# A decoder layer on one core: the folding of the cross-attention weights split between the front and the first tiles, and the order of the front rewritten

## The reference, cut to what matters

```python
x = _layernorm(x + attn(x))            # attn(x) = softmax(rope(q) rope(k)^T * s) v @ w_proj + b_proj + x
# cross attention of the tokens to the context, scale and shift by one number per batch and head
xn = layernorm(ctx, ln1_w, ln1_b); ln = layernorm(x, ln2_w, ln2_b)
q = (ln @ Wq) * (1 + side) + side; k, v = split(xn @ Wkv)
x = _layernorm(x + softmax(q k^T / 8) v @ Wout)
x = _layernorm(x + ffn(x))
```

## Time and profile before

| | us |
|---|---|
| median of 3 runs | 1294.25 |
| lowest, highest | 1291.96, 1299.49 |
| the profiled execution's own time | 1297.17 |
| its span (first to last instruction) | 1295.5 |
| mean granted TensorE clock | 0.91 of full speed |

### The profile page before, as it was taken

How to read it: one execution, slowest core, us unless ns; L and a number is a source line. 1 busy time by engine, 2 the same in 40 slices (tenths; PEclk the granted TensorE clock), 3 DMA queues, 4 the chain that set the end, 5 groups by cost and what they waited for, 6 DMA issues and landing times. The chain is left out here.

```text
span 1295.5 us, 32702 instructions
## 1 busy us (share of the span) xinstructions
PE 1163.4 (90%) x12758; PEld 908.5 (70%) x12762; DVE 1139.7 (88%) x2858; ACT 885.1 (68%) x1248; POOL 622.4 (48%) x520
## 2 busy tenths in 40 slices
PE   6969999999999999999999999999997748888878
PEld 4746777777767777776777777677776628778778
DVE  7768899999989999898999989998986679999984
ACT  4768888888888888888988888898874332222111
POOL 3226667757566775756677575767240300000000
PEclk9779999999999999999999999999998765667666
DMA  8119999999999999999999999998996300000000
GB/s 176 25 47 206 195 193 197 199 183 191 200 206 200 191 203 184 191 206 194 212 184 203 186 196 203 180 186 177 187 188 134 91 1 2 5 6 5 5 5 6
DMA packets 665393, 186.25 MB, mean 144 GB/s; under 512 B 653938, under 2 KB 662294, under 8 KB 664854
## 3 DMA queue, kind: packets, MB, share of 16 engines
q1 hardware_dynamic: 665238, 184.16, 74.7%
HBM read 19.97 MB, written 0.82 MB: 16 GB/s over the span
## 5 line engine op out<-in xcount | busy, mean ns | idle before, releaser
L1174 PE MATMUL ps<-pT,xa_hi 128*128 128x128 f16 x2288 | 380.8, 217 | 20.9 <-ACT uT L1009 20.9
L986 ACT ACTIVATE e<-ps,bias 128x1444 f32<-128x1444 f32 (+1 forms) x208 | 305.8, 1470 | 128.8 <-DVE bias L1058 128.1
L1178 PE MATMUL ps<-pT,xa_hi 128*128 128x128 f16 x2288 | 380.7, 217 | 2.2 <-DMA pT<-p 2.2
L1175 PE MATMUL ps<-pT,xa_lo 128*128 128x128 f16 x2288 | 380.8, 217 | 0.0
L1056 DVE TENSOR_REDUCE nmax<-ps 128x1 f32<-128x1444 f32 (+1 forms) x208 | 343.9, 1653 | 14.1 <-PE ps L1158 13.0
L1068 DVE TENSOR_TENSOR p<-e,p 128x1408 f16<-128x1408 f32 (+3 forms) x288 | 304.4, 1098 | 41.9 <-ACT p L994 41.0
L994 ACT ACTIVATE p<-e 128x1408 f16<-128x1408 f32 (+1 forms) x208 | 288.2, 1385 | 13.9 <-ACT e L986 0.7
L942 POOL TENSOR_TENSOR p<-e,p 128x1408 f16<-128x1408 f32 (+1 forms) x128 | 196.5, 1556 | 181.9 <-ACT p L994 181.9
L1174 PEld LDWEIGHTS ps<-pT,xa_hi 128*128 128x128 f16 x2288 | 222.1, 98 | 48.9 <-issue 36.0
L1156 PE MATMUL ps<-xT_hi,q_hi 128*128 128x512 f16 (+1 forms) x624 | 229.9, 368 | 4.0 <-POOL q_lo L931 3.3
L1175 PEld LDWEIGHTS ps<-pT,xa_lo 128*128 128x128 f16 x2288 | 222.1, 98 | 12.9
(11 more groups left out here) (238 smaller groups left out, 1929.2 us busy)
## 6 DMA issues: line engine op xcount, KB each, us to landing
raw<-in_ctx SPq DMA_DIRECT2D x16, 704.0 KB
pT<-p SPq DMA_TRANSPOSE x416, 3.7
f_wq<-in_L_ffn_w_q SPq DMA_DIRECT2D x1, 1024.0 KB, 5.3
f_wqt<-in_ffn_wq_t SPq DMA_DIRECT2D x2, 512.0 KB, 6.7
raw<-in_ctx SPq DMA_DIRECT2D x48, 18.0 KB
x_tok<-in_x SPq DMA_DIRECT2D x4, 200.0 KB
out_x<-ost SPq DMA_DIRECT2D x6, 128.0 KB, 1.9
wk_t<-in_wk_t SPq DMA_DIRECT2D x1, 512.0 KB, 8.7
```

What stands on the lines that cost most here:

```text
L986: act.activation(e32[t % E_BUF][rows, :], score_banks(t)[rows, 0:T], ACT.Exp, bias=bias[rows, t % N_BUF:t % N_BUF + 1]).then_inc(e_done, 1)
L1174: pe.matmul(out, hi, ph, start=n == 0, stop=False)
L1175: pe.matmul(out, lo, ph, start=False, stop=False)
L1178: pe.matmul(out, hi, pl, start=False, stop=False)
```

## The change

The change rewrites the front and moves work over the first barrier.

- **Self-attention.** `w_proj` is multiplied into the value weights once (`w_vp`, L556), with the bias's part (L557 into `bp_row`). `projected` and its evacuation `oT_out` go. The weights are no longer divided by their sum: `residual` multiplies the finished row by `1/sum` while it adds the input (four instructions per group on DVE). Everything is carried at half scale, so `doubled` becomes an addition on POOL (`biased`). `once_normed` leaves ACT; POOL makes it in slot 2 of each batch (`first_normed`).
- **Key side.** `wk_d` is folded with `fold_k` first, two heads at a time (8 matmuls over 128 rows, `keys_folded`), then 16 matmuls over 64 rows with `wq_t` (`queries_folded`); before it was 16 over 64 rows and 16 over 128. `wk_t` is not loaded any more.
- **Value side.** It leaves the front. Behind the barrier it comes in six pieces of four fp32 matmuls, one in each of slots 1 to 6, each evacuated by ACT (`values_folded`, `values_folded_out`). A piece waits for the evacuation of the one before.
- **Queries of batch 0** are made in the front (`first_queries`, `q0_out`, `q0_hi_out`, `q0_lo`). `FIRST_Q_SLOTS` becomes (7, 9, 10, 11).
- **The second context's statistics** leave DVE's front and stand before its loop in `cross`; its norm, which stood there, moves into slots 1 to 3. The matching power on POOL (`context_rstd`) moves behind the barrier too.
- **POOL** takes over `biased`, `sc1`, `kb`, and the low halves of the normed tokens. The orders of all engines in the front are new, and on SP `w_proj` and `bp_row` come before the first context.

```diff
-Q_SLOTS, FIRST_Q_SLOTS = (1, 6, 9, 10), (5, 6, 9, 10)
+Q_SLOTS, FIRST_Q_SLOTS = (1, 6, 9, 10), (7, 9, 10, 11)
+V_SLOT = 1
+X1_SLOT = 2
...
+            def biased(c):
+                pool.tensor_tensor(out=z[:, of(c), :], in0=x_tok[:, of(c), :], in1=wide(bp_row[:, :], G), op=ALU.add).then_inc(x2b_done, 1)
...
+            def q0_lo(g):
+                cols4 = slice(g * 4 * S, (g + 1) * 4 * S)
+                pool.wait_ge(q0_hi, g + 1)
+                pool.tensor_tensor(out=q_lo[:, cols4], in0=q32[:, cols4], in1=q_hi[:, cols4], op=ALU.subtract)
...
-            def weights(c):
+            def residual(c):
                 dve.wait_ge(exp_done, (c + 1) * G)
-                dve.reciprocal(rc[:, of(c)], rs[:, of(c)]).then_inc(prob_chain, 1)
-                dve.wait_ge(prob_chain, 2 * c + 1)
-                dve.tensor_tensor(out=prob[:, of(c), :], in0=prob[:, of(c), :],
-                                  in1=rc[:, of(c)].rearrange("s (b a) -> s b a", a=1).to_broadcast([S, G, S]),
-                                  op=ALU.mult).then_inc(prob_chain, 1)
+                dve.reciprocal(rc[:, of(c)], rs[:, of(c)]).then_inc(stats_chain, 1)
+                dve.wait_ge(y_ps, c + 1)
+                dve.wait_ge(x2b_done, c + 1)
+                dve.wait_ge(stats_chain, 5 * c + 1)
+                for j in range(G):
+                    b = c * G + j
+                    ins = dve.scalar_tensor_tensor(out=z[:, b, :], in0=bank(c, S, (G, D))[:, j, :], scalar=rc[:, b:b + 1],
+                                                   in1=z[:, b, :], op0=ALU.mult, op1=ALU.add)
+                ins.then_inc(stats_chain, 1)
...
+            def queries_folded(k):
+                pe.wait_ge(rot_chain, rot_count(NG - 1, 1))
+                pe.wait_ge(kf_done, k + 1)
                 for j in range(4):
+                    for half in range(2):
+                        r, rows = 4 * k + j, slice(half * DH, (half + 1) * DH)
+                        last = pe.matmul(qa_bank(2 * k + half)[:, j, :], wq_t[rows, r, :], kf[rows, r, :], start=True, stop=True)
...
-            for part in range(3):
-                context_norm(dve, cx, Batch(None, 1), part)
+            for part in range(4):
+                context_stats(dve, cx, Batch(None, 1), part)
             for t in range(ALL_TILES + DRAIN):
...
+                if 1 <= t <= 3:
+                    context_norm(dve, cx, Batch(None, 1), t - 1)
...
+            def values_folded(k):
+                if k == 0:
+                    pe.wait_ge(ld_v, 32)
+                else:
+                    pe.wait_ge(fv_done, k)
+                for j in range(4):
...
+                last.then_inc(fv_ps, 1)
...
             for t in range(ALL_TILES + DRAIN):
                 if t < ALL_TILES:
                     scores(t)
+                if V_SLOT <= t < V_SLOT + 6:
+                    values_folded(t - V_SLOT)
                 if 0 <= t - LAG < ALL_TILES:
                     values(t - LAG)
```

More of the change, by code:

```diff
@@ new lines, in first_queries @@
+            def first_queries(g):
+                pe.wait_ge(qa_lo_done, 2 if g < 2 else 4)
+                if g == 0:
+                    pe.wait_ge(ln_lo_done, 1)
+                for j in range(4):
+                    out, h = q0_bank(g)[:, j * S:(j + 1) * S], 4 * g + j
+                    pe.matmul(out, qa_hi[:, h, :], ln_hi[:, 0:S], start=True, stop=False)
+                    pe.matmul(out, qa_hi[:, h, :], ln_lo[:, 0:S], start=False, stop=False)
+                    last = pe.matmul(out, qa_lo[:, h, :], ln_hi[:, 0:S], start=False, stop=True)
+                last.then_inc(q0_ps, 1)
@@ L1180, in values @@
                 last.then_inc(pv_done, 1)
-            job("q", 0, 0)
+            def values_folded(k):
+                if k == 0:
+                    pe.wait_ge(ld_v, 32)
+                else:
+                    pe.wait_ge(fv_done, k)
+                for j in range(4):
+                    out = job_bank[:, j * D:(j + 1) * D]
+                    if k < 2:
+                        r = 4 * k + j
+                        last = pe.matmul(out, wv_d[:, 2 * r:2 * r + 2, :].rearrange("d h e -> d (h e)"), fold_v[:, :], start=True, stop=True)
+                    else:
+                        r, half = 4 * ((k - 2) // 2) + j, k % 2
+                        rows = slice(half * DH, (half + 1) * DH)
+                        last = pe.matmul(out, gv[rows, r, :], wout[rows, r, :], start=True, stop=True)
+                last.then_inc(fv_ps, 1)
             for t in range(ALL_TILES + DRAIN):
@@ L1858, in decoder @@
             "kb": sb("kb", [D, B, H], F32, part),
-            "x1": sb("x1", [S, B, D], F32, part),
+            "z": sb("z", [S, B, D], F32, part), "x_mv": sb("x_mv", [S, B, 2], F32, part), "x_rs": sb("x_rs", [S, NG, 2, G], F32, part),
+            "q32": sb("q32", [D, HQ], F32, part),
+            "q_hi": [sb(f"q_hi{i}", [D, HQ], F16, part) for i in range(2)],
+            "q_lo": [sb(f"q_lo{i}", [D, HQ], F16, part) for i in range(2)],
+            "fold_v": sb("fold_v", [D, D], F32, part), "wv_d": sb("wv_d", [D, H, DH], F32, part), "wout": sb("wout", [P, H // 2, D], F32, part),
+            "ld_v": whole.enter_context(nc.semaphore("ld_v")),
         }
```

500 lines of the change are left out of this document (254 added, 246 removed).

## The result

| | before | changed |
|---|---|---|
| median of 20 runs each, us | 1297.39 | 1290.38 |
| lowest, highest | 1291.96, 1299.99 | 1286.74, 1293.65 |
| profiled execution, us | 1297.17 | 1291.46 |
| its span | 1295.5 | 1289.7 |

The ratio of the changed kernel to the one before is 0.9945, 95% interval 0.9935 to 0.9956: 7 us faster. I had forecast 1295.0 and most probably no change. Between the two profiled executions the change brought 5.7 us, where my sum had a loss of 0.7.

A forecast was written before the change was run, and what follows sets the result against it. Front bound by latency chains between PE, ACT and DVE, steady batches by PE. Front -6.0 plus first batch +6.7 gave +0.7 on 1297.17, or 1297.9; less 2.9 for the runs' median, 1295.0; range 1291 to 1300, with rivals 1285 to 1303.

The forecast's parts named there:

- my sum: Whole kernel: 6.0 us gained in the front, 6.7 lost in the first batch, +0.7 on 1297.17.
- The front, before the folding: Front to `twice_normed(0)`: 3.7 us won on DVE, 2.3 left after POOL holds the mix; it ends at 44.3.
- The folding: Key side on PE at half clock: two times eight products at 4.1 us; last `qa_hi` copy at 58.1.
- The weight given to the clock: Front's barrier: 73.0 at half clock until the queries, 66.6 at full; 71.9 taken, 6.0 us gained.
- B: The time the barrier between front and first cross batch opens; 77.87 before, 71.9 forecast.
- the clock holds: Rival for the front: PE idles 1 us only, barrier at 66.6, time 1289.6; chance 0.20.
- one of my own signs of being wrong: Listed sign that the forecast would be wrong: the front ending before 68.
- The tail: Front from last `qa_hi` copy to barrier: 14 to 15 us, as long as before, 11.4 of it ACT's list.
- The first batch: From barrier to tile 13: 69.8 us against 63.1 before, 6.7 lost; bounds 0 and 11.
- the 1.8 us lost at tile 7: First batch: SP's late `turn_high(1)` delays transposes, ACT and value pieces; tile 7 at 37.0 behind the barrier, 35.2 before.
- The wait of 3.6 us for POOL's `q_lo` at tile 13: First batch: the fourth query piece stands behind two norm parts on POOL; expected wait 3 to 5 us.
- an 11 us loss against a gain of 4.9: Rival "Slower": clock falls before tile 13, barrier at 73.0, first batch loses 11 and more; 1301.5, chance 0.15.

The follow-up runs named there:

- halves in turn: Changed kernel with the folding's eight products run as four over rows 0 to 63, then four over rows 64 to 127, not alternating: 0.9982 of the kernel before.
- the filled kernel: Changed kernel plus four unused 128x400 fp32 products on PE in its idle wait for the front's first `twice_normed`: 0.9947 of the kernel before.
- The table of five: Five kernels compared by folding row order, clock and barrier: changed, unedited again, idle stretch filled, halves in turn, both edits; ratios 0.9945, 0.9959, 0.9947, 0.9982, 0.9955.
- the repeat: The changed kernel run once more, unedited, as the measure for its edits: 0.9959 of the kernel before.
- the kernels with a short norm part: Edits of the changed kernel where DVE's first four-tile norm part of context 1 took about 1.11 us; with pieces in the slots, ratios 0.9936 to 0.9982.
- giving POOL a free way: Changed kernel with POOL's norm of context 2 one slot later in the first batch (slots 10, 11, 12): 0.9940 of the kernel before.
- The kernel in turn and filled: Changed kernel with row halves in turn and PE's idle stretch filled with four unused 128x400 fp32 products: 0.9955 of the kernel before.

## Why the prediction was wrong

**The front, before the folding: right.** The last rotation ended at 38.7 (39.5), the conflict moved to the mix (3.19 us for 3.04), `twice_normed(0)` ended at 43.6 (44.3), PE idled 3.4 us (3.3), the clock fell.

**The folding: this is the step that failed.** "Eight products 4.1, the small one 0.5, eight more 4.1" at half clock, with the last `qa_hi` copy at 58.1; it ended at 51.7. Of these 6.4 us, 0.8 are the earlier start. 5.4 are the sixteen products: 8.2 forecast, 2.84 measured. The runs divide that. Eight products at the pace of the row for four are 3.78 at half clock and not 4.1, so two times 0.3 was a wrong scaling: twice the row counts its fixed end twice. Alternating they take 2.08, so two times 1.7 is the pairing, of which halves in turn still have 0.7. The remaining 1.3 us are the clock, which came back at 48.0. Ending them earlier still would not have helped: in the filled kernel they end 1.3 us before that, and the last copy ends at 51.8 all the same. I read the count of products in the diff and took the price from a row of another shape, without asking what the alternation of row halves in the new loop does. The Trainium skill, "TensorE: Matmul & The Clock Gate", "Part 3: Packing small matmuls — row/col tiling", says that products over few rows run at the same time if they lie on different row groups of the array. The trace agrees: the records of the two halves start within 7 ns, and eight products alternating take the time of four on one half, 1.16 for 1.16 at full clock and 2.08 for 2.07 at half.

**The weight given to the clock: wrong in kind.** I gave B = 66.6 for full clock and 71.9 for half, as if PE were the bound. The table of five shows that the clock alone is worth nothing there: the chain of ACT, DVE and POOL sets the barrier as long as the products end by 50.8, as they do in the repeat. The rival "the clock holds" named the right barrier for a wrong reason; the clock did not hold. A front that ended before 68 was one of my own signs of being wrong. The tail had the right length: 14.8 us from the last copy to the barrier (14 to 15), with 11.4 of ACT's list as forecast. The 1 to 2 us of waiting in it were there too (1.6), but for DVE's `shifts` that POOL held and not for PE.

**The first batch: right in sum by luck (6.9 lost, 6.7 forecast), and only partly in its parts.** Tile 7 started at B + 40.3 where I had 37.0, and from there to tile 13 it took 29.6 us where I had 32.8: an error of 3.3 and one of 3.2 us cancel. The value pieces are the main loss, shown by their removal: 6.2 us of offset at tile 13 against the repeat, 3.5 or more against the kernels with a short norm part. I had 4.1 us of net PE time for them. SP's wait released the transpose at B + 23.2, as forecast (22.2 to 24.5), but cost nothing while the pieces were there; the 1.8 us lost at tile 7, which I had led through it, are not its. The wait of 3.6 us for POOL's `q_lo` at tile 13 came as forecast, but giving POOL a free way removed only 0.8 of it, and 1.0 of what was left is DVE's hold on POOL, which I did not have.

**The sum.** -11.3 + 6.9 = -4.5 at tile 13 where I had -6.0 + 6.7. The mechanism of a front given back in part by the first batch was right; one term was off by 5.3 us, nearly the whole error but for 1.3 us behind tile 13. On top of it I took 2.9 us off the sum because the first three runs were low, which hid part of the error: against the median of twenty, 1297.39, my 1295.0 looks like a small gain that the sum did not have. One slip stands in the rivals: an 11 us loss against a gain of 4.9 makes 1300.4 by that way of counting, not 1301.5.

What stays open: among the kernels with value pieces in the slots, those with a short norm part reach tile 13 at B + 66.0 to 67.1 and the changed kernel with its long one at 69.3 to 69.9. So some 2.7 of its 69.9 us go with the race. But the kernel with the filled idle stretch has the long part too and reaches it at 66.9. In these kernels the long part shows as 1.3 to 1.6 us at tile 4 (B + 18.9 to 19.1 for 17.6), and the filled one has made that good by tile 7. Its granted clock is at half once between 75 us and the start of tile 7 (78.3 to 81.7), that of the changed kernel twice (78.7 to 82.1 and 99.2 to 102.6). The kernel in turn and filled has two such stretches (80.4 to 83.8 and 90.6 to 94.0) and the short part, and reaches tile 7 at 37.1. So neither alone costs anything there in these traces, and the changed kernel and its repeat, which are late, have both. No edit tried the race alone with the pieces in the slots, so this share is argued and not shown. It also means that the 6.2 us of the value pieces may be 3.5 of their own and 2.7 of the race.

## What to carry to other kernels

Price a moved or rewritten group of products by how it lies on the array's rows, not by its count, and find out first whether PE or another engine's list ends the stretch: a slower clock costs only where PE is the bound. In a stretch bound by chains, single edits hide one another: SP's wait was worth nothing alone and some 0.4% once the value pieces were out. Take the next wait from the trace of the edited kernel. Where DVE and POOL both work on SBUF, a microsecond upstream decides who is held for three.

## What the runs showed of the hardware

POOL's operations over 128x1408 and 128x1536, 3.1 to 3.3 us long, held on DVE not only a sum of two SBUF operands (3.19 for 0.34) but also `tensor_scalar` with one fp32 SBUF operand (3.65 for 1.11 over four of 128x127; 1.34 for 0.17 over 100x4). The Trainium skill, "SBUF — State Buffer", "Who interferes with whom", says that whichever issues first gets the shared ports for its whole instruction, and counts `tensor_scalar` among those that can use them in a two-port mode, when its operands meet the conditions. The trace agrees: with POOL ahead DVE's norm part lasted until POOL was through. The other order shows at another place: POOL's `q_lo` of 128x400 took 1.81 to 1.94 us instead of 0.94 where DVE's `p` over 128x1408, with two SBUF operands, had begun before it (1.81 in the earlier trace rows).

Eight fp32 products over 64 rows in alternation on the two row halves took as long as four on one half, at either clock level (1.16 and 1.16 us, 2.08 and 2.07), and a third less than the same eight in turn (1.68 and 3.09), which overlap only where one half follows the other.
